# Diagonal score blocks on a mask that ScalarE leaves in PSUM, and the distance product one stage later

## The reference

```
xn = layernorm(x)
s  = gated recurrence over xn, projected, + xn        # layer 0, 512 steps in sequence
g  = silu(tanh(xn @ wo.T + c_final @ uo.T + bo))      # layer 0, a gated cell over the tokens
x  = x + s * g
xn = layernorm(x)
q, k, v = xn @ W, 16 heads of 16                      # layer 1
s  = softmax(causal(q k^T * scale)) v, projected
g  = silu(experts(xn))      # d2 = x2 + p2 - 2 xn @ prototypes.T ; the 2 nearest of 32 are weighed
x  = x + s * g
```

## Time and profile before

| | |
|---|---|
| median of 3 runs (lowest, highest) | 1059.08 us (1058.23, 1061.97) |
| the profiled execution | 1062.24 us, its span 1060.4 us |
| PE, DVE, ACT, POOL busy | 95%, 48%, 48%, 18% of the span |
| granted TensorE clock, mean | 0.984 of full speed |
| `exp`, 128x512, all forms | 320 times, about 600 ns each |
| mask products of the turned scores (L1133) | 320 times |

### The profile page before, as it was taken

One profiled execution on the slowest core, in us unless ns is written; L12 is line 12 of the kernel. 1 busy time (PEld: TensorE's weight loads), 2 busy tenths in 40 slices (PEclk: granted clock), 3 DMA queues, 4 the chain that ended last, 5 costly groups with the idle time before them and its releaser, 6 DMA issues.

```text
span 1060.4 us, 20152 instructions
## 1 busy us (share of the span) xinstructions
PE 1008.4 (95%) x6546; PEld 687.8 (65%) x6546; DVE 506.2 (48%) x1167; ACT 508.2 (48%) x1378; POOL 193.4 (18%) x225
## 2 busy tenths in 40 slices
PE   5999999999999988899999999999999999999986
PEld 3677777777778863564765765765765665665653
DVE  5031123312134464565665665665665566565541
ACT  3344454444444332465465465465465465454433
POOL 5020111101011013213213213213204204200000
PEclk9999999999999996999999999999999999999989
DMA  8422111103100155241451451351362262234110
GB/s 258 146 73 67 59 49 65 45 31 130 38 30 31 41 182 96 100 121 31 135 154 30 123 163 32 107 172 39 96 176 46 78 186 53 70 102 89 31 41 21
DMA packets 66440, 93.79 MB, mean 88 GB/s; under 512 B 11872, under 2 KB 52832, under 8 KB 66400
## 3 DMA queue, kind: packets, MB, share of 16 engines
q1 hardware_dynamic: 60128, 88.83, 29.7%
q10 hardware_dynamic: 6272, 4.46, 1.3%
HBM read 59.41 MB, written 33.59 MB: 88 GB/s over the span
## 4 chain that ended last, share of the span: by engine, by line
PE 84%; DVE 5%; ACT 3%; issue 2%; DMA 1%; ACTq 1%; SPq 0%; POOL 0%; DVEq 0%; POOLq 0%
PE PS L865 26%; PE PS L1146 7%; PE PS L1043 6%; PE PS L1095 6%; PE PS L1076 5%; PE PS L1111 5%; PE PS L852 4%; PE PS L1009 3%; PE PS L1177 3%; DVE nm L1943 3%; PE PS L988 2%; PE PS L1030 2%; PE PS L1097 2%; PE PS L1133 2%; PE PS L1155 1%
## 5 line engine op out<-in xcount | busy, mean ns | idle before, releaser
L865 PE MATMUL PS<-arena 128*128 128x256 f32 x1024 | 314.1, 421 | 0.0
L1943 DVE TENSOR_REDUCE nm<-PS 128x1 f32<-128x512 f32 (+3 forms) x352 | 207.2, 636 | 92.5 <-PE PS L1097 92.4
L1498 ACT ACTIVATE arena<-PS 128x512 f32<-128x512 f32 x256 | 152.2, 600 | 171.7 <-PE PS L1133 170.5
L1344 ACT ACTIVATE arena<-PS 64x8 f32<-64x8 f32 x512 | 88.1, 172 | 193.3 <-PE PS L852 189.9
L852 PEld LDWEIGHTS PS<-arena 128*72 128x72 f32 x1024 | 129.4, 141 | 69.5 <-ACT arena L1344 6.6
L865 PEld LDWEIGHTS PS<-arena 128*128 128x128 f32 x1024 | 155.5, 192 | 0.0
L1111 PE MATMUL PS<-Q,K 98*128 98x512 bf16 (+3 forms) x512 | 120.6, 301 | 8.7 <-ACT arena L1498 4.6
L852 PE MATMUL PS<-arena 128*72 128x8 f32 x1024 | 122.2, 191 | 0.0
L1095 PE MATMUL PS<-K,Q 96*128 96x256 bf16 (+3 forms) x512 | 114.2, 306 | 6.2 <-DMA K<-qk_d 4.5
L1713 DVE SCALAR_TENSOR_TENSOR arena<-arena 128x512 f32<-128x512 f32 x16 | 11.1, 694 | 224.3 <-ACT arena L1355 224.3
L1097 PE MATMUL PS<-negmask,identb 128*128 128x128 bf16 (+2 forms) x352 | 87.4, 248 | 0.0
(11 more groups left out here) (233 smaller groups left out, 1294.8 us busy)
## 6 DMA issues: line engine op xcount, KB each, us to landing
qk_d<-QB SPq DMA_DIRECT2D x24, 512.0 KB, 3.1
Q<-qk_d SPq DMA_DIRECT2D x32, 192.0 KB, 3.7
K<-qk_d SPq DMA_DIRECT2D x32, 192.0 KB, 4.2
gt_d<-arena SPq DMA_DIRECT2D x16, 256.0 KB, 2.5
wx_d<-arena SPq DMA_DIRECT2D x16, 256.0 KB, 2.4
XT<-xt_d SPq DMA_DIRECT2D x8, 512.0 KB, 4.6
GT<-gt_d SPq DMA_DIRECT2D x8, 512.0 KB, 5.9
WX<-wx_d SPq DMA_DIRECT2D x8, 512.0 KB, 6.7
```

Source lines behind the costliest of these rows:

```text
L865: mm = pe.matmul(o, lhs, rhs, start=first, stop=last, skip_group_check=True)
L1344: s_.activation(HB[0:ST, nxt], PS[0:ST, 7, 0:B], ACT.Tanh).then_inc(c_h.sem, 1)
L1498: s_.activation(PR[:, g % 2, j, at:at + T], PS[:, bank, :], ACT.Exp, scale=SCORE_SCALE).then_inc(t_e.sem, 1)
L1943: v_.tensor_reduce(nm[:, g, h:h + n, i], PS[:, u % 3, 0:n * (i + 1) * P].rearrange("p (n w) -> p n w", n=n), AX.X, ALU.max, negate=True).t ...
```

## The change

The turned scores of a group are cut into the ten 128x128 blocks (key tile, query tile) of the causal half, `UNITS`, and step k computes one block for all four heads: four products of 128 columns, each with its own weights. Steps 0, 3, 6 and 8 are the diagonal blocks (`EDGES`). These go to bank 4, the six others to bank 3. The diagonal ones are added (start false) onto a mask that already lies in bank 4. PE writes it once ahead of the loop (`edge_bank`), and from then on ScalarE writes it again after each diagonal `exp` (`write_edge`): behind the side work of steps 0, 3 and 6, and straight behind the `exp` of step 8. A step now waits for the last step before it that used the same bank. A semaphore `t_x` is added, for which `write_edge` waits after its own `exp`. PE's `distance` goes from step 9 of stage 1 to step 0 of stage 2, behind `values`; `take_distance` goes to VectorE's step 3 of stage 2; and in ScalarE's side 8 of stage 1 `take_query_key` 3 now precedes `middle` 0.

```diff
-PU = P_AT[2]
+UNITS = ((0, 0), (0, 1), (0, 2), (1, 1), (0, 3), (1, 2), (2, 2), (1, 3), (3, 3), (2, 3))
+EDGES = tuple(n for n, (kt, q) in enumerate(UNITS) if kt == q)
-TQ = 5 * GH // 2
+TQ = len(UNITS)
+        t_x = count("t_x", G * len(EDGES), 1)
-            def turned_tile(h, kt, bank, at, first):
...
+            def edge_bank():
+
+                pe.wait_ge(c_w.sem, c_w.at(B, 0))
+                pe.matmul(PS[:, 4, :].rearrange("p (n w) -> p n w", n=GH), identb[:, :],
+                          negmask_t[:, :].unsqueeze(1).to_broadcast([P, GH, P]), start=True, stop=True)
             def turned(b, g, k):
                 if k == 0:
                     pe.wait_ge(m_ld[g].sem, m_ld[g].at(b, 2))
-                pe.wait_ge(t_e.sem, t_e.at(b, g * TQ + k - 1))
...
-                pe.matmul(edge, identb[:, :], negmask_t[:, :].unsqueeze(1).to_broadcast([P, n, P]),
-                          start=False, stop=True).then_inc(t_mm.sem, 1)
+                kt, q = UNITS[k]
+                edge = kt == q
+                before = [n - TQ * (n >= k) for n in range(TQ) if (UNITS[n][0] == UNITS[n][1]) == edge]
+                pe.wait_ge(t_e.sem, t_e.at(b, g * TQ + max(before) + 1))
+                for j in range(GH):
+                    h = g * GH + j
+                    mm = pe.matmul(PS[:, 3 + edge, j * P:(j + 1) * P], K6[0:KM, h, kt * P:(kt + 1) * P],
+                                   Q6[0:KM, h, q * P:(q + 1) * P], start=not edge, stop=True,
+                                   skip_group_check=True)
+                mm.then_inc(t_mm.sem, 1)
...
-                    side[9] = [lambda: distance(b + 1)]
...
+                if more:
+                    side[0].append(lambda: distance(b + 1))
...
+            def write_edge(b, g, k):
+
+                act.wait_ge(t_x.sem, t_x.at(b, g * len(EDGES) + EDGES.index(k) + 1))
+                s_.copy(PS[:, 4, :].rearrange("p (j q) -> p j q", q=P),
+                        negmask_t[:, :].unsqueeze(1).to_broadcast([P, GH, P])).then_inc(t_e.sem, 1)
...
                 for k in range(TQ):
                     exp(b, g, k)
+                    if k == EDGES[-1]:
+                        write_edge(b, g, k)
                     run(side, k)
+                    if k in EDGES[:-1]:
+                        write_edge(b, g, k)
...
-                    side[8] = [lambda: middle(b + 1, 0), lambda: take_query_key(b + 1, 3)]
+                    side[8] = [lambda: take_query_key(b + 1, 3), lambda: middle(b + 1, 0)]
...
-                    take_distance(b + 1)
...
+                    side[3] = [lambda: take_distance(b + 1)]
```

More of the change, by code:

```diff
@@ L1106, in maxima_turn @@
                              ).then_inc(m_t.sem, 1)
-            def turned_tile(h, kt, bank, at, first):
-                w = T - kt * P
-                pe.matmul(PS[:, bank, at:at + w], K6[0:KM, h, kt * P:(kt + 1) * P],
-                          Q6[0:KM, h, kt * P:T], start=first, stop=False)
+            def edge_bank():
+                pe.wait_ge(c_w.sem, c_w.at(B, 0))
+                pe.matmul(PS[:, 4, :].rearrange("p (n w) -> p n w", n=GH), identb[:, :],
+                          negmask_t[:, :].unsqueeze(1).to_broadcast([P, GH, P]), start=True, stop=True)
             def turned(b, g, k):
@@ L1276, in _ @@
             maxima_turn(0, 0)
+            edge_bank()
             pe.wait_ge(y_v.sem, y_v.at(1, 2))
@@ L1303, in _ @@
             s_ = nc.scalar
-            for s in (b_xt, b_ue, c_h, c_t, g_t, n_x2, n_xt, q_e, q_1, d_e, h_e, e_t, t_e, o_e, r_e, x_n, g_h, m_a, n_xn,
+            for s in (b_xt, b_ue, c_h, c_t, g_t, t_x, n_x2, n_xt, q_e, q_1, d_e, h_e, e_t, t_e, o_e, r_e, x_n, g_h, m_a, n_xn,
                       w_e):
@@ L1490, in exp @@
                 act.wait_ge(t_mm.sem, t_mm.at(b, g * TQ + k + 1))
[L1491 to L1499, removed]
+                kt, q = UNITS[k]
+                at = P_AT[kt] + (q - kt) * P
+                bank = PS[:, 3 + (kt == q), :].rearrange("p (j q) -> p j q", q=P)
+                s_.activation(PR[:, g % 2, :, at:at + P], bank, ACT.Exp, scale=SCORE_SCALE
+                              ).then_inc((t_x if kt == q else t_e).sem, 1)
+            def write_edge(b, g, k):
+                act.wait_ge(t_x.sem, t_x.at(b, g * len(EDGES) + EDGES.index(k) + 1))
+                s_.copy(PS[:, 4, :].rearrange("p (j q) -> p j q", q=P),
+                        negmask_t[:, :].unsqueeze(1).to_broadcast([P, GH, P])).then_inc(t_e.sem, 1)
             def take_values(b, g):
```

## The result

The kernel after takes 1077.97 us (median of 4 runs, 1071.02 to 1080.8), the kernel before, run beside it, 1060.38 us. The ratio is 1.0159, with a 95% interval of 1.0128 to 1.019. So the change costs about 17 us. It was predicted to cost 6. The profiled execution took 1080.8 us with a span of 1078.8 us; it is the longest of the four. The profiled execution of before, 1062.24 us, stood above its median too, by less.

A forecast was written before the change was run, and what follows sets the result against it. PE, busy 95% of the span, was taken to bound the kernel. Terms 4.9 - 0.3 - 0.8 + 2.1 + 0.2 = +6.1 us on a median of 1059.1 gave 1065 us, range 1044 to 1083.

The forecast's parts named there:

- the forecast's own range: Whole kernel: 1060 to 1071 us, the span given for case A.
- case B: Rival: clock falls at stage ends, 7 of 15 places at 2.5 us each, 1082 us; chance 0.18.
- The products of 128 columns: Turned scores on PE: four products in a row, each with its own weights, take 0.22 us, the full rate.
- The copy: ScalarE's mask write into PSUM: next instruction 0.49 us after its start, bounds 0.24 and 0.65; four per stage.
- Stage 1 into 2: PE waits for mask copy and `exp` 9, where `distance` had filled the time; step 1 of stage 2 0.95 us later.
- Stage 2 into 3: `exp` 9 delayed behind the mask copy, `second_odds` and `open_gate`; `values` at 39.5 us, +0.8.
- Stage 3 into 0: Mask copies of steps 6 and 8 delay ScalarE's queue; `values` +1.25 us.
- An image: Net over one image's four stages: +0.7 us, counted seven times for +4.9 us.
- The last stage: Stage 3 of the last image, a ScalarE chain: step 1 to `values` 8.9 us instead of 6.8, +2.1.
- the clock holds: TensorE's granted clock does not fall at the new stage-end waits; assumed by case A.
- case A: The forecast: copies hidden except at three stage ends of an image, clock unchanged, 1060 to 1071 us; chance 0.42.
- Case C: Rival: copies between `exp` 6 and `exp` 9 on ScalarE's queue cost next to nothing, about 1048 us; chance 0.30, not slower.

The follow-up runs named there:

- experiment 8: The changed kernel with `distance` back in stage 1 and PE adding the mask, one 512-column product per diagonal step, no mask copies: 1058.39 us, ratio 0.9987.
- experiment 5: The kernel before with only `distance` moved behind `values` of stage 2, with the reordering that goes with it: 1065.26 us, ratio 1.0038.
- experiment 1: The changed kernel with idle products (five, three, six, two) in PE's waits at the ends of stages 1 and 3: 1092.08 us, ratio 1.0284.
- experiment 2: The changed kernel with fewer idle products (two, one, three, one) in PE's waits at the ends of stages 1 and 3: 1069.04 us, ratio 1.0068.
- experiment 6: The changed kernel with no mask on the turned scores and no mask copies, diagonal `exp` at a hundredth of the scale: 1053.93 us, ratio 0.9934.
- experiment 3: The changed kernel with `distance` and `take_distance` back in stage 1, mask copies kept: 1078.25 us, ratio 1.0148.
- experiment 7: The changed kernel with `distance` back in stage 1 and VectorE writing the masks in place of ScalarE: 1075.97 us, ratio 1.0132.
- experiment 9: The changed kernel with `distance` back in stage 1; ScalarE copies masks for steps 3 and 6 only, PE adds those of 8 and 0: 1057.21 us, ratio 0.9982.
- experiment 10: As experiment 9, but with `distance` behind `values` of stage 2 as in the changed kernel: 1060.77 us, ratio 1.0011.

## Why the prediction was right, and where it was not

The direction was right, the size was not: +6 us forecast, +17 measured. The measured 1078 us lies 7 us above the forecast's own range, 1060 to 1071. It lies in the wide range, 1044 to 1083, only because that one reached up to case B. By its steps:

- **The products of 128 columns** were taken at 0.22 us for four. In after, the step at 708.72 is followed by a score at 708.95, 0.23 us later. Right, and experiment 8 prices it over the whole kernel. The 81 ns per product of the Trainium skill ("TensorE: Matmul & The Clock Gate", section "Back-to-back issue gap") do not hold for these groups: by an estimate from that figure experiment 8 would stand some 33 us higher.
- **The copy** was taken at 0.49 us, within bounds of 0.24 to 0.65. It is 589 ns long, and the next instruction comes 0.53 us after its start (708.07 to 708.60). From `exp` 8 to the instruction behind the copy it is 1.16 us; 1.14 was forecast.
- **Stage 1 into 2.** Step 2 waits: its distance from step 1 (694.23) is 1.09 us, 1.13 forecast. From step 0 of stage 1, step 0 of stage 2 was forecast at 18.0, `values` at 19.9 and step 1 at 24.0; they came at 17.93, 19.88 and 23.98. Right, and so is the cause as written, that `distance` had filled the time in which PE now waits: in experiment 5, with no copies, the move alone costs 0.74 us per image.
- **Stage 2 into 3.** `values` forecast at 39.5, measured 730.32 - 690.79 = 39.53. Right.
- **Stage 3 into 0.** The order and the waits are as forecast, the low-rank copy at 57.06 (747.85 - 690.79) against 57.03. The wait for the mask copy in front of step 0 is 1.32 us (1.20 to 1.55 in the other images). Behind one of these the clock stayed low the longest, from 751 to 758 us.
- **An image**: +0.7 forecast, +0.79 where the clock holds.
- **The last stage**: step 1 to `values` forecast 8.9 us, measured 1061.55 - 1052.63 = 8.92. What the sum didn't have is that the last `values` and the tail then run at the lower clock, 4.00 us for `values` in place of 2.36; from their start to the end of the kernel it is 1.6 us more than before.

**The step that failed is "the clock holds" in case A.** Case B was written as an alternative to A and came on top of it. It named the mechanism, the places and about their number (7 of 15 places forecast, 7 in the six images of this execution), at a chance of 0.18, and its sign, a granted clock of 0.5 in the middle of images, came. The argument against it was that PE does a microsecond of work between the two waits and that the shorter waits of today cost no clock. The runs show that this work is not enough: experiments 1 and 2 fill the standstill and the falls inside images are gone. The price per fall was 2.5 us and is 1.5 to 1.6 in the mean. One reason is in its source: it came from the `values` of 4.36 us in the earlier trace rows, and six of the seven in after took 3.95 to 4.05. Another may be that a fall makes PE slower just when it would stand and wait for `exp` 9, so that part of it is hidden; no run isolates this. Of the two errors one made the other look smaller: with seven falls at 2.5 us case B came to 1082. With experiment 2 as the kernel after with a held clock, the sum is 7 for the schedule (forecast 6.1) and 9 to 10 for the clock.

I should have asked of the profile which stretches of before come near the fall, and not only whether there is one. Between its first image and its last `values` before had one fall, at the wait of the earlier trace rows. The forecast put two waits, 2 us in sum, at the end of every stage 1 and 2.6 us at every stage 3, where before stood still for 0.30 us ahead of `distance`, and at the end of stage 3 for 0.72 us ahead of step 0 and 0.26 us ahead of `values`. The prediction's picture of PE leaves out the 0.72 us:

```profile
660.49 0.39 PE L1111 MATMUL PS<-Q,K 98*128 98x512 bf16 x1 [0.72 <-ACT arena L1498]
```

The Trainium skill describes such a thing on its page "TensorE: Matmul & The Clock Gate", section "A second HAM failure mode: psum-queue depth-cycling": a TensorE that stands still for short moments between groups of products can swing between its two clock levels, and the throughput is lost there, not in the length of a single product. The trace agrees: waits of 0.42 to 1.55 us, with products between them, came ahead of every fall inside images, the `values` outside the low stretches kept their 2.36 us. But the same waits also stood at stage ends without a fall. The forecast had not weighed this section.

**Case C** was the likeliest way to a kernel that is not slower. Its place was right, its price is refuted by the copy's own rows and by experiment 6: the copies, exposed or not, cost 2.07 us per image.

**What stays open.** Why the clock falls at some of the stage ends and not at others with the same waits. And why, with `distance` in the wait, it fell at ends of stage 1 in experiments 3 and 7, but not in the kernel before or in experiment 9, where `distance` stands in the same place. The wait in front of it is about 0.3 us in these two and in experiment 8, and about 0.5 in experiments 3 and 7, but the first images of experiment 7 had that wait without a fall; no run isolates the reason.

## What to carry to other kernels

Removing work from the busiest engine pays only up to the next thing it waits for: here masks that cost nothing returned 7 of 28.8 us with `distance` moved, and would have returned an estimated 11 without. Before moving work onto another engine's queue, walk through the stage ends, where nothing hides that queue, and leave the old way in place there (experiments 9 and 10 do, and are the only versions with copies that are not clearly slower than before). Independent work that stands in front of a wait, as `distance` did, is already the filling. And add the new waits up by place: here two or three of 0.4 to 1.5 us close together cost TensorE's clock at seven of twelve stage ends, and that was worth more than the waits. Which of them fall could not be told ahead.

## What the runs showed of the hardware

- The granted clock fell to 0.50 behind stage ends at which PE's longest single wait was 1.09 to 1.55 us (seven times in six images of after). Three or four idle f32 products per place kept it up inside the images (experiment 2).
- ScalarE's copy from SBUF into PSUM, 128x512 from bf16 to f32, takes 589 ns (x128), no less than its copy out of PSUM, 0.58 to 0.59 us; VectorE's takes 683 ns (x128).
- An idle f32 product of 256 columns costs PE 0.44 us and is recorded as two.
